# VectorE's side work of an iteration's second place behind the next iteration's q bias

## The chip, the cores and the metric

The kernel runs on one core of one Trainium2 chip. The metric is the device time of one execution in microseconds (us), lower is better. The time of the kernel before is 2167.18 us, the median of 3 runs (2166.52 to 2167.47). One more execution was taken by the hardware profiler; it took 2164.84 us, and its span, from the first to the last recorded instruction, is 2163.1 us.

## What is computed

One block of a network with adaptive layer norm: an attention-like layer and a mixture-of-experts layer, both with a residual, on 16 x 256 tokens of width 256, all in float32. What matters here, cut from the reference:

```python
h = _layernorm(x) * (1 + ca) + sa
q = (h @ q_w.T + q_b); k = (h @ k_w.T + k_b); v = (h @ v_w.T + v_b)   # 16 heads of 128
beta = softplus(h @ b_w.T + b_b)
qn, kn = _l2norm(q / scale), _l2norm(k / scale); gv = beta[..., None] * v
attn = einsum('bnhid,bnhjd->bnhij', qc, kc)                            # chunks of 64 tokens
out = einsum('bnhij,bnhjd->bnhid', attn * mask, gvc) * silu(h @ og_w.T)
x = x + ga * (out @ o_w.T + o_b)
h = _layernorm(x) * (1 + cb) + sb
scores = softmax(h @ gate_w.T); topk_w, topk_ids = lax.top_k(scores, 6)
x = x + gb * (sum over 16 experts of combine * swiglu(h) + shared swiglu(h))
```

## The kernel before

The tokens are cut into 32 tiles of 128, and 4 tiles make a supertile of 512. The 16 heads are cut into 4 groups of 4. The first phase, attention, is one loop over n = 0 to 127 (and two more turns to drain): iteration n treats one token tile t = n mod 4 of a supertile for one group of heads. The phase takes the first 1320 us or so. The second phase, experts, follows and is not touched.

Each engine has its own queue, in which the instructions stand in the order of the code, and semaphores join the queues. In iteration n TensorE does, in this order: the q projection of tile n (6 matmuls, 512 columns each), side work of the first place, the k projection, the output projection of the last supertile if t is 2, the scores of n-1 (`score(n - 1)`, into `s_ps`), the v projection, the attention product (`attend(n - 1)`, into `av_ps`), the transposes of q and k (`qt_ps`, `kt_ps`), side work of the second place, and, if t is 1, four gate projections (`project_gate`, 6 matmuls each). The q, k, v and gate products share two PSUM banks, `proj_ps0` and `proj_ps1`, in turn: `bank_free` makes each product wait until the one two before it has been read. So the v projection waits for the q bias, the second gate product waits for the v bias, and the third for ScalarE's silu of the first.

VectorE reads the products and adds the biases (`add_bias`, L1428: q, k, v), masks the scores (`mask`, L1434), makes the low part of the gated output (`lo_part`, L1457), the guarded sums of squares (`sum_squares`, L1441), and applies the gate (`apply_gate`, L1449). ScalarE squares q and k (L1117), copies the transposed q and k (L1108, L1110), makes the high part (`hi_part`, L1125, after L1449), and the silu of the gate products (L1131). GpSimd takes the inverse square root (L608) and scales q (L611) and v (L620).

Side work is what the main loop does not need at once: the layer norms of later supertiles, the preparation of later weights, and the routing for the experts. `plan()` puts it by a table of numbers into `side[n, 0]` and `side[n, 1]`, the first and the second place of iteration n, and each engine does its share of a task where its queue comes to that place. For VectorE the kinds with work of its own are, of the second places:

- `prep` and `tile` (a transposed piece of weights, 512 or 256 columns): TensorE transposes it into a PSUM bank, ScalarE copies the high part into `stage` (L1071), VectorE subtracts for the low part (L1335), waits for its own result and frees the bank, and SyncE stores the stage to memory (L398). There are two stage buffers, and the high part of a piece waits until the store of the piece two before it has landed.
- `stats`: `bn_stats` x4 (L1210), `bn_aggr` x4 (L1214), and an addition of eps (L1218), each waiting for the one before. GpSimd takes the inverse root (L592), and `norm` (L1227), in the first place of the next iteration, needs it.
- `x1` (L1284), the residual; `zturn` (L1250, L1256), the start of the softplus; `one` (L1261).

In the rows a tensor is named without its number: `q_sb`, `k_sb`, `v_sb` are the results of the biases, `scores<-s_ps` is the mask, and `proj_ps<-h_t,w_gate` a gate product.

Of the kernel before, what the change touches and what calls it, by code (L numbers as in the profile page):

```python
# [18 lines left out]
TS = ST // P  # L19
# [23 lines left out]
N = NI * TS  # L43
# [3 lines left out]
def after(eng, sem, count):  # L47
    if count > 0:
        eng.wait_ge(sem, count)


def f32(ap):
    return ap.bitcast(FP32)
# [81 lines left out]
def build(nc, x, q_w, q_b, k_w, k_b, v_w, v_b, b_w, b_b, og_w, o_w, o_b, gate_w, w13, w2, sw13, sw2, c, wmod, out):  # L135
    ctx = ExitStack()
    with ctx:
# [139 lines left out]
        side, late = plan()  # L277
# [921 lines left out]
        def _(dve):  # L1199
# [155 lines left out]
            n = KC * B  # L1355
# [14 lines left out]
            def boot_part(kind, h):  # L1370
                j = 2 * kind + h
                to = w_qkv[:, 0, kind, h] if kind < 3 else (w_gate if kind == G else w_out)[:, h]
                dve.wait_ge(boot_hi, j + 1)
                dve.tensor_tensor(to[:, 1, :], boot_ps[j][:, :], f32(to[:, 0, :]), ALU.subtract).then_inc(boot_lo, 1)
# [21 lines left out]
            def late_modulation():  # L1396
                dve.wait_ge(mod_turned, 2)
                dve.tensor_copy(mod[:, 4:12, :], s_ps[:, 2 * P:4 * P].rearrange("p (r d b) -> p r d b", r=8, d=2)[:, :, 0, :])\
                   .then_inc(gained, 1)
                dve.wait_ge(made, 3)  # L1400
                dve.wait_ge(gained, 3)
                gain = mod[:, CB * KC:(CB + 1) * KC, :]
                dve.tensor_scalar(gain, gain, 1.0, None, ALU.add).then_inc(gained, 1)
                steps = 4
                for w in (GA, GB):
                    m, s = mod[:, w * KC:(w + 1) * KC, :], sign[:, :, :]
                    dve.wait_ge(gained, steps)
                    dve.tensor_scalar(s, m, 0.0, 2.0, ALU.is_ge, ALU.mult).then_inc(gained, 1)
                    dve.wait_ge(gained, steps + 1)
                    dve.scalar_tensor_tensor(out=m, in0=m, scalar=-1.0, in1=m, op0=ALU.mult, op1=ALU.max).then_inc(gained, 1)  # L1410
                    dve.wait_ge(gained, steps + 2)
                    dve.tensor_scalar(m, m, 0.25, None, ALU.max).then_inc(gained, 1)
                    dve.wait_ge(gained, steps + 3)
                    dve.scalar_tensor_tensor(out=m, in0=s, scalar=-1.0, in1=m, op0=ALU.add, op1=ALU.mult).then_inc(gained, 1)
                    steps += 4
                dve.wait_ge(gained, steps)
                for h in range(KC):
                    dve.tensor_scalar(ga_ob[:, h, :], mod[:, GA * KC + h, :], o_b_sb[:, h:h + 1], None, ALU.mult)\
                       .then_inc(gained, 1)

            def add_bias(n, what):
                i, t = divmod(n, TS)
                if what == Q and n % 8 == 0:
                    dve.wait_ge(bias_loaded[(n // 8) % 2], 48 * (n // 16 + 1))
                dve.wait_ge(projected[what], n + 1)
                after(dve, (q_turned, k_turned, attended)[what], n - 1)
                at = (t + what) % 2
                dve.tensor_tensor(raw[what][t % 2][:, :], proj_ps[at][:, :], bias[:, (i // 2) % 2, what, :], ALU.add)\  # L1428
                   .then_inc(biased[what], 1)

            def mask(n):
                dve.wait_ge(scored, n)
                after(dve, attended, n - 1)
                dve.tensor_tensor(heads(scores[:, :]), heads(s_ps[:, :]),  # L1434
                                  causal[:, :].unsqueeze(1).broadcast_to([P, HG, P]), ALU.mult).then_inc(masked, 1)

            def sum_squares(n):
                dve.wait_ge(q_squared, n + 1)
                dve.wait_ge(k_squared, n + 1)
                after(dve, inverted, n - 1)  # L1440
                dve.tensor_scalar(guarded[n % 2][:, :], sumsq[n % 2][:, :], NORM_EPS2, None, ALU.max).then_inc(guard_done, 1)  # L1441

            def apply_gate(n):
                i, t = divmod(n - 1, TS)
                dve.wait_ge(attended, n)
                dve.wait_ge(gate_ready, HG * (i + 1))
                after(dve, gated_hi_done, n - 2)
                after(dve, gated_lo_done, n - 2)
                dve.tensor_tensor(gated[t % 2][:, :, :], heads(av_ps[:, :]), gate[:, :, t * P:(t + 1) * P], ALU.mult)\  # L1449
                   .then_inc(gated_done, 1)  # L1450

            def lo_part(n):
                i, t = divmod(n - 1, TS)
                at = slice(t * P, (t + 1) * P)
                dve.wait_ge(gated_hi_done, n)
                after(dve, out_projected, 2 * i)
                dve.tensor_tensor(gated_lo[:, :, at], gated[t % 2][:, :, :], f32(gated_hi[:, :, at]), ALU.subtract)\  # L1457
                   .then_inc(gated_lo_done, 1)

            def add_out(i, h):  # L1460
                g, a = group(i), i % 2
                dve.wait_ge(out_projected, 2 * i + h + 1)
                sums = acc[:, h, a * ST:(a + 1) * ST]
                if g == 0:
                    after(dve, delta_done, supertile(i) - 1)
                    dve.tensor_copy(sums, out_ps[:, :]).then_inc(added, 1)
                else:
                    dve.wait_ge(added, 2 * (i - 2) + h + 1)
                    dve.tensor_tensor(sums, out_ps[:, :], sums, ALU.add).then_inc(added, 1)
# [11 lines left out]
            def weigh(u):  # L1481
                w, a = divmod(u, 2)
                q, m = divmod(w, NM)
                dve.wait_ge(silu_done, u + 1)
                if m < ME:
                    if m == 0 and a == 0:
                        dve.wait_ge(comb_loaded[q % 2], 32 * (q // 2 + 1))
                    dve.tensor_tensor(silu_g[a][:, :], silu_g[a][:, :], combine[q % 2][:, a, :], ALU.mult)\
                       .then_inc(weighted, 1)

            def multiply(u):
                w, a = divmod(u, 2)
                q, m = divmod(w, NM)
                if m < ME:
                    dve.wait_ge(weighted, 2 * (q * ME + m) + a + 1)
                dve.wait_ge(u_done, u + 1)
                after(dve, hid_hi_done, u - 1)
                after(dve, hid_lo_done, u - 1)
                dve.tensor_tensor(hid[a], up_bank(u)[:, :], silu_g[a][:, :], ALU.mult).then_inc(hid_done, 1)  # L1499

            def lo_hidden(u):
                a = u % 2
                dve.wait_ge(hid_hi_done, u + 1)
                after(dve, downed, u - 1)
                dve.tensor_tensor(hid_lo[a], hid[a], f32(hid_hi[a]), ALU.subtract).then_inc(hid_lo_done, 1)

            for n in range(N + 2):
                i, t = divmod(n, TS)
                if n < N:
                    add_bias(n, Q)  # L1510
                    add_bias(n, K)
                if t == 2 and i:
                    add_out(i - 1, 0)
                if n == N + 1:
                    lo_hidden(0)
                if n >= 2:
                    mask(n - 1)
                if t != 2 and n >= 3:
                    lo_part(n - 2)
                if n >= N:  # L1520
                    weigh(n - N)
                if n < N:
                    for task in side[n, 0]:
                        do(task)
                    add_bias(n, V)
                    sum_squares(n)
                if t == 2 and i:
                    add_out(i - 1, 1)
                if n >= 2:
                    apply_gate(n - 1)  # L1530
                if n >= N:
                    multiply(n - N)
                if t == 1 and n >= 2:
                    lo_part(n - 1)
                if n == 1:
                    for h in range(KC):
                        boot_part(O, h)
                    late_modulation()
                if n < N:
                    for task in side[n, 1]:  # L1540
                        do(task)
                if n == 0:
                    for h in range(KC):
                        boot_part(G, h)
# [42 lines left out]
```

## Time and profile before

| | |
|---|---|
| median of 3 runs | 2167.18 us |
| profiled execution | 2164.84 us, span 2163.1 us |
| TensorE matmul busy | 2135.4 us, 99% of the span |
| TensorE weight load busy | 1752.6 us, 81% |
| VectorE busy | 1154.5 us, 53% |
| ScalarE busy | 1031.5 us, 48% |
| GpSimd busy | 522.2 us, 24% |
| granted TensorE clock | 1.0 of full speed (2.4 GHz) |

Busy time is what the instructions of an engine cover; matmuls are pipelined and overlap, so a busy TensorE may still have small holes in its rhythm. A time row reads: start, duration, engine, line, operation, what it writes and reads, count, and in brackets the idle time before it and what ended that. Where instructions follow each other without a wait, the next one starts before the recorded end of the one before (by some 0.08 us on VectorE), so the distance of two starts is what one really takes.

### The profile page before, as it was taken

The page shows a single profiled execution, that of the slowest core. Times are in us where ns is not written, and L with a number is a line of the kernel's source. Part 1 is how long each engine was busy: PE and PEld are TensorE (multiplying, and loading weights), DVE is VectorE, ACT ScalarE, POOL GpSimd, SP SyncE. Part 2 cuts the span into 40 slices and gives each one's busy share as a digit, 9 for nine tenths or more (in the row PEclk, how much of TensorE's full clock was granted, in tenths as well). Part 3 has the DMA queues.
Part 4 walks back from the last instruction along what each step waited for, and adds up shares of the span by engine and source line. Part 5 has one row for each costly group of instructions (what it writes and reads, how often), then busy time and mean ns, then how long its engine had stood idle before and what let it go on. Part 6 is the DMA issues. An engine that isn't in the chain of part 4 may idle for free.

```text
span 2163.1 us, 36173 instructions
## 1 busy us (share of the span) xinstructions
PE 2135.4 (99%) x12463; PEld 1752.6 (81%) x12463; DVE 1154.5 (53%) x2174; ACT 1031.5 (48%) x3300; POOL 522.2 (24%) x540
## 2 busy tenths in 40 slices
PE   8999999999999999999999999999999999999999
PEld 6778888888888887878888888888888888888887
DVE  6555654555555555555554445555555455545554
ACT  6655664665665665565565453333332333333232
POOL 2433443443443343343343441000000000000000
PEclk9999999999999999999999999999999999999999
DMA  8574443254355354354233221342334234323221
GB/s 264 185 239 133 146 138 123 81 162 139 93 145 159 84 154 136 95 147 142 106 143 113 70 107 49 129 170 98 127 125 149 88 121 156 103 97 113 96 94 63
DMA packets 191892, 274.79 MB, mean 127 GB/s; under 512 B 99184, under 2 KB 132960, under 8 KB 191712
## 3 DMA queue, kind: packets, MB, share of 16 engines
q1 hardware_dynamic: 191712, 272.49, 39.6%
q8 instruction: 101, 1.65, 0.3%
q14 instruction: 79, 0.65, 0.1%
HBM read 214.79 MB, written 57.67 MB: 126 GB/s over the span
## 4 chain that ended last, share of the span: by engine, by line
PE 92%; DVE 3%; ACT 2%; issue 2%; DMA 1%; DVEq 0%; POOL 0%; SPq 0%; ACTq 0%; POOLq 0%
PE proj_ps L651 49%; PE out_ps L651 14%; PE av_ps L877 5%; PE s_ps L866 4%; PE s_ps L924 3%; PE av_ps L924 3%; PE qt_ps L924 3%; PE kt_ps L924 3%; PE qt_ps L847 2%; PE kt_ps L852 2%; DMA head_scr<-stage 1%; PE misc_ps L670 1%; PE out_ps L721 0%; ACT squares L1117 0%; PE misc_ps L679 0%
## 5 line engine op out<-in xcount | busy, mean ns | idle before, releaser
L651 PE MATMUL proj_ps<-w_qkv,h_t 128*128 128x512 f32 x2304 | 618.0, 406 | 10.3 <-DVE q_sb L1428 2.1
L651 PEld LDWEIGHTS proj_ps<-w_qkv,h_t 128*128 128x128 f32 x2304 | 407.9, 188 | 103.3 <-issue 20.2
L651 PE MATMUL proj_ps<-h_t,w_qkv 128*128 128x512 f32 x1800 | 444.2, 391 | 0.3 <-issue 0.2
L651 PEld LDWEIGHTS proj_ps<-h_t,w_qkv 128*128 128x128 f32 x1800 | 335.6, 188 | 70.2 <-issue 1.3
L608 POOL TENSOR_TENSOR inv_norm<-guarded,minus_half 128x8 f32<-128x8 f32 x128 | 209.4, 1636 | 741.9 <-DVE guarded L1441 741.9
L1108 ACT ACTIVATE q_t<-qt_ps 128x512 f32<-128x512 f32 x128 | 76.3, 596 | 303.9 <-PE qt_ps L847 303.4
L651 PE MATMUL proj_ps<-h_t,w_gate 128*128 128x512 f32 x768 | 190.2, 398 | 2.6 <-ACT gate L1131 1.3
L1428 DVE TENSOR_TENSOR v_sb<-proj_ps,bias 128x512 f32<-128x512 f32 x128 | 88.5, 691 | 190.0 <-PE av_ps L877 183.4
L1117 ACT ACTIVATE squares<-q_sb 128x128 f32<-128x128 f32 x512 | 151.4, 297 | 56.9 <-DVE q_sb L1428 52.4
L1428 DVE TENSOR_TENSOR q_sb<-proj_ps,bias 128x512 f32<-128x512 f32 x128 | 88.4, 690 | 165.5 <-PE proj_ps L651 160.7
L651 PEld LDWEIGHTS proj_ps<-h_t,w_gate 128*128 128x128 f32 x768 | 139.8, 188 | 40.2 <-ACT gate L1131 10.7
L1117 ACT ACTIVATE squares<-k_sb 128x128 f32<-128x128 f32 x512 | 151.1, 297 | 19.8 <-DVE k_sb L1428 18.2
L651 PE MATMUL out_ps<-gated_hi,w_out 128*128 128x512 f32 x512 | 158.0, 390 | 0.1
L651 PE MATMUL out_ps<-h_t,w_qkv 128*128 128x512 f32 x594 | 150.9, 389 | 0.0
L1428 DVE TENSOR_TENSOR k_sb<-proj_ps,bias 128x512 f32<-128x512 f32 x128 | 88.4, 690 | 116.1 <-PE proj_ps L651 115.7
L877 PEld LDWEIGHTS av_ps<-scores,v_sb 128*128 128x128 f32 x1024 | 133.9, 191 | 10.7
L1151 ACT ACTIVATE w_gate<-v_sb 128x512 fp32r<-128x512 f32 x100 | 63.2, 632 | 161.8 <-DVE v_sb L1499 161.8
L1151 ACT ACTIVATE w_gate<-squares 128x512 fp32r<-128x512 f32 x100 | 63.2, 632 | 158.8 <-DVE squares L1499 154.6
L620 POOL TENSOR_TENSOR v_sb<-v_sb,v_scale 128x512 f32<-128x512 f32 x128 | 135.6, 1059 | 10.0
L611 POOL TENSOR_TENSOR q_sb<-q_sb,inv_norm 128x512 f32<-128x512 f32 x128 | 135.2, 1056 | 10.0
L877 PE MATMUL av_ps<-scores,v_sb 128*128 128x128 f32 x1024 | 134.7, 274 | 0.0
L651 PEld LDWEIGHTS out_ps<-h_t,w_qkv 128*128 128x128 f32 x594 | 111.5, 188 | 23.5
(216 smaller groups left out, 3174.5 us busy)
## 6 DMA issues: line engine op xcount, KB each, us to landing
w_qkv<-tile_scr SPq DMA_DIRECT2D x100, 768.0 KB, 4.3
w_qkv<-head_scr SPq DMA_DIRECT2D x45, 1024.0 KB, 11.0
head_scr<-stage SPq DMA_DIRECT2D x30, 512.0 KB, 3.8
w_gate<-head_scr SPq DMA_DIRECT2D x15, 1024.0 KB, 4.9
w_out<-head_scr SPq DMA_DIRECT2D x15, 1024.0 KB, 4.9
tile_scr<-stage SPq DMA_DIRECT2D x25, 512.0 KB, 3.1
x_in<-_attn_hidden_states_dram SPq DMA_DIRECT2D x16, 512.0 KB, 6.7
h_scr<-stage SPq DMA_DIRECT2D x16, 512.0 KB, 3.3
```

The lines of the kernel that those rows point to most:

```text
L608: pool.tensor_tensor(inv_norm[b][:, :], guarded[b][:, :], minus_half[:, :], ALU.pow).then_inc(inverted, 1)
L611: pool.tensor_tensor(q, q, inv_norm[b][:, 0:HG].unsqueeze(2).broadcast_to([P, HG, P]), ALU.mult)\
L620: pool.tensor_tensor(v, v, v_scale[b][:, :].unsqueeze(2).broadcast_to([P, HG, P]), ALU.mult)\
L651: mm = pe.matmul(out, w, y, start=(j == 0 and m == 0), stop=(3 * j + m == n - 1))
L847: mm = pe.transpose(qt_ps[:, h * P:(h + 1) * P], raw[Q][b][:, h * P:(h + 1) * P], ident)
L866: mm = pe.matmul(s_ps[c * CH:(c + 1) * CH, at], k_t[:, at], q_t[:, at], start=True, stop=True)
L877: mm = pe.matmul(av_ps[:, at], raw[V][(n - 1) % 2][:, at], scores[:, at], start=True, stop=True)
L924: mm = pe.matmul(y_ps[a][h][:, :], tiles_w[:, w % 4, r, at], y, start=(m == 0 and j == 0), stop=(m == NM - 1 and j == 2))
L1108: act.activation(q_t[:, :], qt_ps[:, :], ACT.Copy).then_inc(qt_copied, 1)
L1117: m = act.activation(squares[:, what, at], raw[what][n % 2][:, at], ACT.Square, accum_out=sumsq[n % 2][:, what * HG + h:what * HG + h + 1])
L1151: act.activation(hid_hi[u % 2], hid[u % 2], ACT.Copy).then_inc(hid_hi_done, 1)
L1428: dve.tensor_tensor(raw[what][t % 2][:, :], proj_ps[at][:, :], bias[:, (i // 2) % 2, what, :], ALU.add)\
```

## The change

VectorE's share of the second place of iteration n moves from the end of iteration n to the next iteration, between its q bias and its k bias, for all n from 2 to 126 but those with n mod 4 = 1. Nothing is added or taken away, and no other engine's order changes.

```diff
+            behind_q = lambda n: 2 <= n < N - 1 and n % TS != 1
             for n in range(N + 2):
                 i, t = divmod(n, TS)
                 if n < N:
                     add_bias(n, Q)
+                    if behind_q(n - 1):
+                        for task in side[n - 1, 1]:
+                            do(task)
                     add_bias(n, K)
...
-                if n < N:
+                if n < N and not behind_q(n):
                     for task in side[n, 1]:
                         do(task)
```

With the table as it is, 33 of the moved places hold work for VectorE: 10 a `prep` alone and one a `prep` with `one`, 3 a `tile`, 7 a `zturn`, 6 an `x1`, and 6 the `stats` of a routing norm, 5 of these with a `tile` behind it. The `stats` are those of n = 32, 40, 64, 72, 96 and 104, so their new place lies in iterations 33, 41, 65, 73, 97 and 105, which have t = 1 and so the gate products.

VectorE's queue from the end of iteration 40 into iteration 41, before:

```order
430 L1449 TENSOR_TENSOR gated<-av_ps,gate 128x512
431 L1210 BN_STATS stats<-x_in 128x6 x4
432 L1214 BN_AGGR mean_var<-stats 128x2 x4
433 L1218 TENSOR_SCALAR var_eps<-mean_var 128x4
434 L1335 TENSOR_TENSOR stage<-misc_ps,stage 128x256
435 L1428 TENSOR_TENSOR q_sb<-proj_ps,bias 128x512
436 L1428 TENSOR_TENSOR k_sb<-proj_ps,bias 128x512
437 L1434 TENSOR_TENSOR scores<-s_ps,causal 128x512
438 L1457 TENSOR_TENSOR gated_lo<-gated,gated_hi 128x4x128
439 L1227 TENSOR_SCALAR xn<-x_in,mean_var,rstd 128x256 x4
440 L1335 TENSOR_TENSOR stage<-out_ps,stage 128x512
441 L1428 TENSOR_TENSOR v_sb<-proj_ps,bias 128x512
```

The same place in the changed kernel:

```order
430 L1449 TENSOR_TENSOR gated<-av_ps,gate 128x512
431 L1428 TENSOR_TENSOR q_sb<-proj_ps,bias 128x512
432 L1210 BN_STATS stats<-x_in 128x6 x4
433 L1214 BN_AGGR mean_var<-stats 128x2 x4
434 L1218 TENSOR_SCALAR var_eps<-mean_var 128x4
435 L1335 TENSOR_TENSOR stage<-misc_ps,stage 128x256
436 L1428 TENSOR_TENSOR k_sb<-proj_ps,bias 128x512
437 L1434 TENSOR_TENSOR scores<-s_ps,causal 128x512
438 L1457 TENSOR_TENSOR gated_lo<-gated,gated_hi 128x4x128
439 L1227 TENSOR_SCALAR xn<-x_in,mean_var,rstd 128x256 x4
440 L1335 TENSOR_TENSOR stage<-out_ps,stage 128x512
441 L1428 TENSOR_TENSOR v_sb<-proj_ps,bias 128x512
```

The q bias moved ahead of the three steps of the statistics and the tile's low part, which now stand between it and the k bias.

The end of iteration 23 and the start of 24, where only a `prep` moves, before:

```order
268 L1449 TENSOR_TENSOR gated<-av_ps,gate 128x512
269 L1335 TENSOR_TENSOR stage<-misc_ps,stage 128x512
270 L1428 TENSOR_TENSOR q_sb<-proj_ps,bias 128x512
271 L1428 TENSOR_TENSOR k_sb<-proj_ps,bias 128x512
272 L1434 TENSOR_TENSOR scores<-s_ps,causal 128x512
```

And in the changed kernel:

```order
268 L1449 TENSOR_TENSOR gated<-av_ps,gate 128x512
269 L1428 TENSOR_TENSOR q_sb<-proj_ps,bias 128x512
270 L1335 TENSOR_TENSOR stage<-misc_ps,stage 128x512
271 L1428 TENSOR_TENSOR k_sb<-proj_ps,bias 128x512
272 L1434 TENSOR_TENSOR scores<-s_ps,causal 128x512
```

The q bias and the low part of the stage have changed places, and the rest stands as it was.

## Rows read from the trace of the kernel before

**Rows 1.** The page: busy time, share and count of each engine.
```profile
PE 2135.4 (99%) x12463; PEld 1752.6 (81%) x12463; DVE 1154.5 (53%) x2174; ACT 1031.5 (48%) x3300; POOL 522.2 (24%) x540
```
**Rows 2.** Waits of TensorE: who waited, for whom, us in total, times, longest.
```profile
PE proj_ps L651 <- DVE q_sb L1428: 2.1, 3, 1.1
```
**Rows 3.** Timeline of VectorE and TensorE around the start of iteration 24.
```profile
269.79 0.69 DVE L1335 TENSOR_TENSOR stage<-misc_ps,stage 128x512 fp32r<-128x512 f32 x1 [1.18 <-ACT stage L1071]
270.72 0.69 DVE L1428 TENSOR_TENSOR q_sb<-proj_ps,bias 128x512 f32<-128x512 f32 x1 [0.24 <-DVE stage L1335]
...
271.56 1.63 PE L651 MATMUL proj_ps<-w_qkv,h_t 128*128 128x512 f32 x6 [0.58 <-DVE q_sb L1428]
```
**Rows 4.** Timeline of VectorE, end of iteration 40 and iteration 41.
```profile
435.32 1.40 DVE L1210 BATCH_NORM_STATS2 stats<-x_in 128x6 f32<-128x256 f32 x4
...
437.16 0.51 DVE L1218 TENSOR_SCALAR var_eps<-mean_var 128x4 f32<-128x4 f32 x1
...
438.21 0.69 DVE L1428 TENSOR_TENSOR q_sb<-proj_ps,bias 128x512 f32<-128x512 f32 x1 [0.21 <-DVE stage L1335]
438.82 0.68 DVE L1428 TENSOR_TENSOR k_sb<-proj_ps,bias 128x512 f32<-128x512 f32 x1
...
442.80 0.69 DVE L1428 TENSOR_TENSOR v_sb<-proj_ps,bias 128x512 f32<-128x512 f32 x1 [0.21 <-DVE stage L1335]
```
**Rows 5.** Timeline of TensorE, iteration 41 and the start of 42.
```profile
436.64 0.60 PE L721 MATMUL out_ps<-ident,nat 128*128 128x128 f32 x4
...
438.57 0.69 PE L866 MATMUL s_ps<-q_t,k_t 128*64 128x64 f32 x16
...
440.68 1.05 PE L877 MATMUL av_ps<-scores,v_sb 128*128 128x128 f32 x8
...
442.36 1.17 PE L651 MATMUL proj_ps<-h_t,w_gate 128*128 128x512 f32 x4
...
448.26 1.07 PE L651 MATMUL proj_ps<-w_qkv,h_t 128*128 128x512 f32 x4
```
**Rows 6.** Timeline of ScalarE, iteration 41.
```profile
444.73 1.27 ACT L1131 ACTIVATE gate<-proj_ps 128x512 f32<-128x512 f32 x2
```
**Rows 7.** Timeline of GpSimd, iteration 41; lines L1218, L1256: ns min/median/max.
```profile
436.61 1.04 POOL L611 TENSOR_TENSOR q_sb<-q_sb,inv_norm 128x512 f32<-128x512 f32 x1
...
437.88 1.04 POOL L620 TENSOR_TENSOR v_sb<-v_sb,v_scale 128x512 f32<-128x512 f32 x1
...
L1218 DVE TENSOR_SCALAR var_eps<-mean_var x16: 169/170/506, 6.9 to 1482.9; 128x4 f32<-128x4 f32 x16
...
L1256 DVE SCALAR_TENSOR_TENSOR soft<-z x8: 225/226/1095, 20.6 to 954.5; 128x64 f32<-128x64 f32 x8
```
**Rows 8.** Timeline, statistics and side transposes of iterations 65 and 33.
```profile
680.61 1.40 DVE L1210 BATCH_NORM_STATS2 stats<-x_in 128x6 f32<-128x256 f32 x4
...
681.76 0.38 PE L721 MATMUL out_ps<-ident,nat 128*128 128x128 f32 x2
...
354.04 1.40 DVE L1210 BATCH_NORM_STATS2 stats<-x_in 128x6 f32<-128x256 f32 x4
...
354.75 0.60 PE L721 MATMUL out_ps<-ident,nat 128*128 128x128 f32 x4
```
**Rows 9.** Timeline of VectorE, TensorE, SyncE and ScalarE, iterations 7 to 9.
```profile
97.25 0.69 DVE L1335 TENSOR_TENSOR stage<-misc_ps,stage 128x512 fp32r<-128x512 f32 x1 [1.18 <-ACT stage L1071]
98.19 0.69 DVE L1428 TENSOR_TENSOR q_sb<-proj_ps,bias 128x512 f32<-128x512 f32 x1 [0.24 <-PE proj_ps L651]
...
97.89 0.60 PE L709 MATMUL out_ps<-ident,nat 128*128 128x128 f32 x4
...
98.02 0.33 SPq L398 DMA_DIRECT2D head_scr<-stage  x1
...
103.31 0.37 SPq L381 DMA_DIRECT2D w_gate<-head_scr  x1
...
110.16 0.60 ACT L1071 ACTIVATE stage<-out_ps 128x512 fp32r<-128x512 f32 x1 [3.03 <-DMA head_scr<-stage]
```

## The prediction

> **What bounds the kernel now.** I read the page first. TensorE's matmuls cover 99% of the span, VectorE's work 53% [rows 1]. So VectorE's order matters only where TensorE waits for it. The second view is TensorE's waits. Of the q bias, which the change lets go earlier, it has three waits, 2.1 us in all, the longest 1.1 [rows 2]. That is all that an earlier q bias can give back: 0.1% of the time. The third view is the timeline around the moved places, since what is late there after the change is no wait yet.
>
> **Where the q bias is late now.** At the start of iteration 24 the low part of a stage waits 1.18 us for ScalarE, runs from 269.79, and the q bias follows only at 270.72. The v projection, which needs its bank, starts at 271.56 after 0.58 us of idle time [rows 3]. This pair gives two prices. A low part holds the queue for 0.93 us up to the next bias (its length and the wait for its own end before it frees the bank). And TensorE starts 0.84 us after the start of the VectorE instruction that releases it.
>
> **The prep and tile places (14), x1 (6), zturn (7).** A q bias that finds VectorE free starts about 0.3 us after its projection ends: the side transposes behind the projection of iteration 8 start at 97.89, the bias at 98.19 [rows 9]; I take 0.25. In iteration 41 the q projection ends at 436.64 and the k projection at 438.57 [rows 5], 1.93 us apart with side transposes between. In this gap fit the q bias (0.61, the distance of two biases, 438.21 to 438.82, [rows 4]) and a low part of 0.93. The k bias is then on time, or, where no transposes stand in the gap or the high part is late, up to 0.3 late. It may be 0.56 late at no cost: on time, at 438.57 + 0.11, its mask would start at 439.28, and the attention product at 440.68 [rows 5] needs it only by 440.68 - 0.84 = 439.84. So in the low-part places nothing is lost on TensorE by the k bias. Iteration 24 gains the 0.58, iteration 16, by the same pattern, I take as 0.2. Sum -0.8, bounds 0 and -2.1. x1 is an instruction of a low part's shape, and zturn is shorter; both cost nothing, as they fit in the gap.
>
> For zturn a row speaks against that. Its second step (L1256) took 0.23 in the median, but once 1.09 us [rows 7]. After the move it stands where GpSimd scales q, and if it waits each time for that (1.04 us, [rows 7]) the k bias is up to 0.1 later than the slack allows: 7 times 0.1, 0.7 us, the upper bound. I take 0. The Trainium skill ("SBUF — State Buffer", "Who interferes with whom") says that a VectorE instruction with two inputs in SBUF waits out a GpSimd instruction that reads SBUF and started first. By that rule, the wait would come in all seven; the 1.09 agrees with it.
>
> **The six statistics places.** Here lies the cost. At the end of iteration 40 VectorE is free at 435.32 and uses the time in which TensorE still does the q projection: the statistics start at 435.32, and statistics and low part are done when the q bias starts at 438.21, 2.89 us later [rows 4]. The q bias is already 1.3 late, but it costs TensorE nothing: the v projection runs on time. After the change VectorE has nothing to do from 435.32 until the q projection's end plus 0.25, 436.89: it idles 1.57 us, and then has the same work to do before the v bias. From 435.32 to the v bias at 442.80 its queue is full but for two waits of 0.21 for its own results [rows 4]. So the v bias comes 1.57 us later, less what the work itself gets shorter.
>
> It does get shorter by one item. The addition of eps took 0.51 us at 437.16, against a median of 0.17 [rows 7]; it ended at 437.67, when GpSimd's scaling of q, started at 436.61, ended (437.65). In its new place it starts at 436.89 + 0.61 + 1.84 = 439.34 (1.84 from 435.32 to 437.16), and GpSimd's next long one has ended at 438.92 [rows 7]. That saves 0.34.
>
> What hangs on it on TensorE: first the attention product. New mask: 436.89 + 0.61 + (2.89 - 0.34) + 0.60 = 440.65, so the product starts at 441.49 instead of 440.68, 0.8 late. Then the gate products. They start at 442.36 and the next iteration at 448.26 [rows 5]: 5.90 for four, 1.47 each if none waits, and the third would start at 445.30. But the third needs the bank that ScalarE's silu of the first reads, and that hangs on a chain: v bias 442.80, sums of squares, gate, ScalarE's high part, silu at 444.73 for 0.64 [rows 6], which is 445.37. So the end of iteration 41 hangs on the v bias with no slack, and moves by its whole 1.57 - 0.34 = 1.23 us. The 0.8 of the attention product is inside that and not added.
>
> The other five by the same count. Idle time added, from the start of the statistics to the start of the side transposes plus 0.25 [rows 8]: iteration 65 has 1.40, 33 has 0.96; 73 is like 65, and 97 and 105 like 41. Sum 3 x 1.57 + 2 x 1.40 + 0.96 = 8.5. Less 5 x 0.34; in 33 the eps meets GpSimd's scaling of v again and I count 0.2: 1.9. Net +6.6. Bounds: 8.5 if nothing is saved; 4.6 if only the attention product waits (3 x 0.8, 2 x 0.87, 0.46).
>
> **The stores behind the moved low parts.** SyncE's queue is in order. The low part of iteration 7's prep starts at 97.25 now, and behind the q bias it starts at 98.19 + 0.61 = 98.80, 1.55 later. Its store (98.02) goes with it, so does the w_gate load at 103.31, which waits for the store to land, and the store behind that load; ScalarE in iteration 9 waited 3.03 us, until 110.16, for a stage buffer [rows 9]. It would wait until 111.7, and with it v bias and gate products of iteration 9: +1.5. The other preps move by 0 to 0.5, since their low parts wait for the high part anyway, as in [rows 3]; one more chain of this kind, in iteration 13, I take as +0.5. Sum +2.0, bounds 0 (a store lands faster when fewer transfers are beside it) and +4. No other engine's order changes; the phase of the experts, 840 us, is as before.
>
> **Sum.** -0.8 + 6.6 + 2.0 = +7.8 us. Against its own time, 2164.84 for the profiled execution, that is 2172.6. That execution is 2.3 below the median of the runs; on the median of 2167.18 the forecast is 2175.0 us, 0.36% slower. What a measurement of this kernel can tell from no change is about 0.2%, 4.3 us: slower means above 2171.5, faster below 2162.8.
>
> **Rivals.**
> - *The freed q bias is all that counts (not slower).* If the gate products do not hang on the v bias, and the attention product has more slack than I read, the statistics cost nothing and the waits of [rows 2] go: -1.2 with the stores at 0, 2166.0; at most -2.1, 2165.1. For it: a q bias 1.3 late costs nothing now, so a late k bias may also. Against: the k bias would be 436.89 + 0.61 + 2.55 = 440.05, 1.37 late against a slack of 0.56, and the mask stands directly behind it. It decides from side work of under 1.8 us in the gap; the statistics with a tile have 2.55. 0.15, of which 0.03 is faster.
> - *Only the attention product waits.* The third gate product has slack that the merged rows hide: 4.6 instead of 6.6, stores and gains as before or less, +4 to +6; 2172 on the median. For it: that the third product waits for the silu is worked out, not read. 0.17.
> - *The stage stores pile up.* In the first 280 us the two stage buffers are turned twice an iteration, and TensorE also waits for weights there. If each of the 11 moved preps hands on a delay, +4 more than forecast, and eps saves nothing, +1.9: +14, 2181. Against: only one low part moves by more than 0.5. 0.10.
> - The forecast, +6 to +10: 0.58.
>
> Faster 0.03, within 0.2% 0.20 (the rest of the first, and 0.08 of the second and of the forecast's lower edge), slower 0.77. Range 2169.0 to 2179.0: below it lie the first rival, above it the worst of the third.
>
> **What the new profile would show.** Right: in iteration 41 and its five like, TensorE's attention product waits 0.5 to 0.9 us for the mask, a wait that the list of waits does not have now, and the gate products wait for ScalarE's silu; VectorE idles about 1.5 us before the q bias there; the eps addition is 0.17 in five of six; the 0.58 of iteration 24 is gone; in iteration 9 ScalarE waits some 4.5 us for its stage. Wrong: the v bias of iteration 41 not later than its q projection by 1.2 more than now; or the gate products not moved by it; or a second phase that changes by more than 0.5 us.

## The result, and the profile after

The changed kernel takes 2172.59 us (median of 8 runs, 2172.11 to 2173.72), the kernel before 2166.20 us in the same runs (median of 8, 2164.82 to 2167.47). The ratio is 1.0031, with a 95% interval of 1.0020 to 1.0041: 6.4 us slower (+4.3 to +8.9 by the interval), which the scatter of the runs does not explain. The forecast was +7.8 us and 2175.0 us; on this median of the kernel before it would be 2174.0. The profiled execution of the changed kernel took 2172.43 us (span 2170.7).

The page after, the same line as [rows 1]; nothing in it says why the kernel is slower:

```profile
PE 2136.8 (98%) x12463; PEld 1751.3 (81%) x12463; DVE 1154.1 (53%) x2174; ACT 1031.1 (48%) x3300; POOL 522.5 (24%) x540
```

The waits of TensorE say more (the changed kernel; who waited, for whom, us in total, times, longest):

```profile
PE proj_ps L651 <- ACT gate L1131: 3.3, 11, 1.2
PE av_ps L877 <- DVE scores L1434: 2.8, 5, 0.6
PE proj_ps L651 <- DMA w_qkv<-head_scr: 1.6, 1, 1.6
...
PE proj_ps L651 <- DVE q_sb L1428: 1.1, 1, 1.1
```

Of the 2.1 us of waits for the q bias in [rows 2], 1.1 are left, the one of the start-up. In their place stand five waits of the attention product for the mask, which were not in the list before, and 3.3 us for the silu of the gate products. Before, that line was:

```profile
PE proj_ps L651 <- ACT gate L1131: 1.3, 6, 0.4
```

Most of the growth on that line lies elsewhere: 1.8 of the 3.3 us are two waits in iterations 9 and 13, and four of the six statistics iterations (33, 41, 73, 97) have one of 0.16 to 0.18 us each. The list shows only a wait of over 0.15 us, and from the recorded end of the matmuls before, so what the silu costs has to be read from distances of starts, below.

The timeline of VectorE in iteration 41, the answer to [rows 4] (start, duration):

```profile
438.66 0.69 DVE L1428 TENSOR_TENSOR q_sb<-proj_ps,bias 128x512 f32<-128x512 f32 x1 [1.43 <-PE proj_ps L651]
439.27 1.40 DVE L1210 BATCH_NORM_STATS2 stats<-x_in 128x6 f32<-128x256 f32 x4
440.70 0.38 DVE L1214 BATCH_NORM_AGGREGATE mean_var<-stats 128x2 f32<-128x6 f32 x4
441.12 0.17 DVE L1218 TENSOR_SCALAR var_eps<-mean_var 128x4 f32<-128x4 f32 x1
441.19 0.42 DVE L1335 TENSOR_TENSOR stage<-misc_ps,stage 128x256 fp32r<-128x256 f32 x1
441.82 0.69 DVE L1428 TENSOR_TENSOR k_sb<-proj_ps,bias 128x512 f32<-128x512 f32 x1 [0.21 <-DVE stage L1335]
442.43 0.68 DVE L1434 TENSOR_TENSOR scores<-s_ps,causal 128x512 f32<-128x512 f32 x1
...
445.82 0.69 DVE L1428 TENSOR_TENSOR v_sb<-proj_ps,bias 128x512 f32<-128x512 f32 x1 [0.21 <-DVE stage L1335]
```

VectorE idles 1.43 us before the q bias (1.5 by the distance of starts), in the time in which it did the statistics before. The eps addition takes 0.17 us now, not 0.51, since no GpSimd instruction lies over it. And from the start of the statistics to the v bias the queue is full again.

TensorE in the same iteration, the answer to [rows 5]:

```profile
438.46 0.60 PE L721 MATMUL out_ps<-ident,nat 128*128 128x128 f32 x4
...
440.39 0.69 PE L866 MATMUL s_ps<-q_t,k_t 128*64 128x64 f32 x16
...
443.17 1.16 PE L877 MATMUL av_ps<-scores,v_sb 128*128 128x128 f32 x8 [0.50 <-DVE scores L1434]
...
444.96 3.27 PE L651 MATMUL proj_ps<-h_t,w_gate 128*128 128x512 f32 x12
448.39 3.02 PE L651 MATMUL proj_ps<-h_t,w_gate 128*128 128x512 f32 x12 [0.16 <-ACT gate L1131]
451.24 1.07 PE L651 MATMUL proj_ps<-w_qkv,h_t 128*128 128x512 f32 x4
```

From the side transposes behind the q projection to the first product of the next iteration it was 448.26 - 436.64 = 11.62 us, and it is 451.24 - 438.46 = 12.78: 1.16 us more in this one iteration. Of these, the attention product has 0.67 before its start (443.17 - 440.39 = 2.78, against 440.68 - 438.57 = 2.11) and 0.11 from there to the first gate product (1.79 against 1.68), and the four gate products have 0.38 (451.24 - 444.96 = 6.28, against 448.26 - 442.36 = 5.90). Note that the bracket of the attention product says 0.50 and not 0.67: an idle time is counted from the recorded end of the matmuls before, which overlap.

What held the gate products can be read from single matmuls. The second product of the changed kernel, and the third product of the kernel before (each from a window that opens inside it; the count is that of the window), are:

```profile
446.57 1.66 PE L651 MATMUL proj_ps<-h_t,w_gate 128*128 128x512 f32 x6
```

```profile
445.37 1.45 PE L651 MATMUL proj_ps<-h_t,w_gate 128*128 128x512 f32 x5
```

The second product starts 446.57 - 445.82 = 0.75 us after the start of the v bias, and 0.38 us after the matmul before it, where two matmuls of one product are 0.23 apart. The third starts 448.39 - 447.75 = 0.64 us after the start of the silu:

```profile
447.75 1.11 ACT L1131 ACTIVATE gate<-proj_ps 128x512 f32<-128x512 f32 x2
```

In the kernel before it was 445.37 - 444.73 = 0.64 too, and 0.39 after the matmul before it. In all six statistics iterations of both kernels the silu starts 1.93 us after the v bias, and the third product 0.63 to 0.64 after the silu. So the third product hung on the v bias with no slack before the change and does so after it.

The same difference can be taken for every iteration: how much later the scores of the iteration after it start than before. The steps over 0.08 us are these (us, positive is later), each profile against that of the kernel before:

| step behind iteration | changed kernel | only statistics (e2) | without statistics (e1) |
|---|---|---|---|
| 1 (start-up, no place moved) | -0.90 | -0.13 | 0 |
| 7 to 9 | +1.41 | +0.46 | +1.28 |
| 12 and 13 | +1.25 | +1.02 | -0.48 |
| 15, 16 | -0.06 | 0 | -0.13 |
| 24 | -0.61 | 0 | -0.61 |
| 33 | +0.67 | +0.68 | 0 |
| 41 | +1.17 | +1.16 | 0 |
| 65 | +1.00 | +1.01 | 0 |
| 73 | +1.06 | +1.06 | 0 |
| 97 | +1.29 | +1.24 | 0 |
| 105 | +1.19 | +1.20 | 0 |

The six statistics places have 6.4 us, and behind iteration 105 the distance stays as it is to the end of the phase. The profiled executions as a whole are 7.6 us apart. The other 1.2 us come before iteration 25: +1.8 up to iteration 13, where e2, still equal to the kernel before, has +1.4, and -0.6 in iteration 24.

### The profile page after: what moved, and what is told of

It is laid out like the page before. It is cut to its first block, busy times and chain, and to the rows that moved or that the text cites. A ratio compares the mean times of both kernels' runs of the same rounds, so it can differ in the third digit from the quotient of the medians.

```text
span 2170.7 us, 36173 instructions
## 1 busy us (share of the span) xinstructions
PE 2136.8 (98%) x12463; PEld 1751.3 (81%) x12463; DVE 1154.1 (53%) x2174; ACT 1031.1 (48%) x3300; POOL 522.5 (24%) x540
## 4 chain that ended last, share of the span: by engine, by line
PE 89%; DVE 4%; ACT 2%; issue 2%; DMA 1%; SPq 0%; DVEq 0%; ACTq 0%
PE proj_ps L651 48%; PE out_ps L651 14%; PE av_ps L877 5%; PE s_ps L866 3%; PE s_ps L924 3%; PE av_ps L924 3%; PE qt_ps L924 3%; PE kt_ps L924 3%; PE qt_ps L847 2%; PE kt_ps L852 2%; DMA head_scr<-stage 1%; PE misc_ps L670 1%; ACT gate L1131 1%; DVE stage L1335 0%; DVE xn L1227 0%
```

## The experiments

The theory to test: the loss lies in the six statistics places alone. VectorE idles there before the q bias and does the work after it, in front of the k bias, the mask and the v bias, and the gate products hang on the v bias over a chain. Rivals: any side work between q and k bias costs something; the loss is in the stores of the first 280 us; only the mask is waited for.

**e1, without the statistics places.**

```diff
-            behind_q = lambda n: 2 <= n < N - 1 and n % TS != 1
+            behind_q = lambda n: 2 <= n < N - 1 and n % TS != 1 and not any(task[0] == "stats" for task in side[n, 1])
```

> The changed kernel with the six places that hold the statistics left where they were before; the other 27 moved. My theory: all but about 1.4 us of the loss (the stores behind the moved low parts, less the freed q bias) goes, and the attention products of iterations 33, 41, 65, 73, 97, 105 wait for no mask: 0 to +2.5 us against before. A rival, that any side work between the q bias and the k bias costs something, says at least +4.

Measured: 2165.30 us against 2165.74 of the kernel before, ratio 0.9996 (0.9988 to 1.0005). The loss is gone with the six places; the other 27 moved places together cost nothing that can be measured, in the median 0.4 us less than before (-2.6 to +1.1), a little below the 0 to +2.5 that I expected. The rival's +4 lies outside the interval, and no wait of the attention product for the mask is in the list.

**e2, the statistics places alone.**

```diff
+            behind_q = lambda n: 2 <= n < N - 1 and any(task[0] == "stats" for task in side[n, 1])
```

> Only the six statistics places are moved (n = 32, 40, 64, 72, 96, 104), everything else as before. My theory: +6.4 us against before, of which iteration 33 has 0.7 and the others 1.0 to 1.3 each, and nothing before 350 us. The rival that the loss is in the stores of the first 280 us says under +3.

Measured: 2171.90 us against 2165.74, ratio 1.0028 (1.0017 to 1.0039), +6.2 us. The table above shows the same six steps as in the changed kernel, each within 0.05 us. One part of the expectation missed: the profile has steps of +1.5 us behind iterations 7 to 13 too, where this kernel is word for word the kernel before. More on this under e5.

**e6, only the tile behind the q bias.** In five of the places the statistics stay, and the tile's low part moves:

```diff
+            behind_q = lambda n, task: 2 <= n < N - 1 and task[0] == "tile" and side[n, 1][0][0] == "stats"
...
+                    for task in side.get((n - 1, 1), ()):
+                        if behind_q(n - 1, task):
+                            do(task)
                     add_bias(n, K)
...
                     for task in side[n, 1]:
-                        do(task)
+                        if not behind_q(n, task):
+                            do(task)
```

> In five of the six places the statistics stay at the end of the iteration and only the tile's low part goes behind the q bias; everything else as before. My theory (VectorE loses time only where it idles before the q bias, and the k bias may be 0.56 us late): VectorE idles nowhere, the queue up to the v bias is as full as before, 0 us, within 0.5 of before. The rival that a late k bias costs by itself says +0.5 us per place, +2.5.

Measured: 2165.45 us against 2165.74, ratio 1.0000 (0.9991 to 1.0008). Its VectorE timeline in iteration 41:

```profile
435.69 1.39 DVE L1210 BATCH_NORM_STATS2 stats<-x_in 128x6 f32<-128x256 f32 x4
...
437.95 0.68 DVE L1428 TENSOR_TENSOR q_sb<-proj_ps,bias 128x512 f32<-128x512 f32 x1
438.55 0.41 DVE L1335 TENSOR_TENSOR stage<-misc_ps,stage 128x256 fp32r<-128x256 f32 x1
439.17 0.69 DVE L1428 TENSOR_TENSOR k_sb<-proj_ps,bias 128x512 f32<-128x512 f32 x1 [0.21 <-PE proj_ps L651]
...
443.17 0.69 DVE L1428 TENSOR_TENSOR v_sb<-proj_ps,bias 128x512 f32<-128x512 f32 x1 [0.21 <-DVE stage L1335]
```

From the statistics to the v bias it is 443.17 - 435.69 = 7.48 us, as before (442.80 - 435.32 = 7.48, [rows 4]). So a low part behind the q bias costs nothing as long as the queue stays full ahead of it. The run says nothing of a late k bias: against the end of the q projection the k bias starts here at 439.17 - 437.01 = 2.16 us, and in the kernel before at 438.82 - 436.64 = 2.18, so it did not get later, and the rival of the expectation was not put to the test.

**e3, the chain behind the v bias, taken by itself.** The kernel before, with the silu of the first gate product ahead of the high part on ScalarE:

```diff
+                first = 1 if t == 1 and 2 <= n < N else 0
+                if first:
+                    silu_gate(i, 0)
                 if n >= 2:
                     hi_part(n - 1)
...
-                    for h in range(HG):
+                    for h in range(first, HG):
                         silu_gate(i, h)
```

> The kernel before, with one other change: in the iterations with gate products (t = 1, n of 5 and more) ScalarE does the silu of the first gate product ahead of the high part, not behind it. My theory says that the third gate product waits on the chain v bias, gate, high part, silu, not only in the six places but by about 0.3 us in most of these iterations (5.82 us for four products in the middle, 5.53 at best). Then this takes 0.54 us out of the chain, and the kernel gets faster by 31 x 0.3 = 9 us at most, 5 to 9 us. If the gate products are not bound by that chain, nothing changes (within 1 us).

Measured: 2160.10 us against 2165.74, ratio 0.9974 (0.9964 to 0.9985): 5.6 us faster. The chain from the v bias over gate, high part and silu is real, and held TensorE in the kernel before as well. It held it in fewer iterations than the 31 I had multiplied: the profile has steps of -0.2 to -0.4 us behind 33, 37, 41, 45, 65, 69, 73, 77, 97, 101, 105 and 109, where VectorE has side work ahead of the v bias, and next to none in the others. These are 4.3 us, which is what the two profiled executions differ by; the rest of the 5.6 is not seen in the one profile. That the total fell into the range of 5 to 9 us is in part luck, since 31 iterations were counted on and 12 gained.

**e4, the changed kernel with e3's edit.**

> The changed kernel together with the silu of the first gate product ahead of the high part. If the gate products hang on v bias, gate, high part and silu in the statistics iterations, the freed 0.54 us is partly usable there too: each is then bound by the attention product (+0.8) and by the second gate product's wait for the v bias (+0.3), so +1.1 each against the kernel with the silu first alone, 6 us in all, 2166 us; a wait of the gate products for the v bias appears in their place. If they hung on the attention product alone, the loss would be 4.6.

Measured: 2165.19 us against 2165.33, ratio 0.9999 (0.9990 to 1.0008). e3 ran in another session; each against its own kernel before, this one is 5.5 us above e3. Step by step against e3's profile: 0.51, 1.08, 0.85, 0.90, 1.15 and 1.07 in the six iterations, 5.6 in sum, against 6.4 without the edit. So part of the loss hung on the silu, as the theory says, and the larger part comes by the attention product. The wait for the v bias that I expected in its place is not in the list of waits, but it shows in the starts. TensorE in iteration 41, and below it the second product by itself:

```profile
440.98 1.16 PE L877 MATMUL av_ps<-scores,v_sb 128*128 128x128 f32 x8 [0.51 <-DVE scores L1437]
...
442.76 6.00 PE L651 MATMUL proj_ps<-h_t,w_gate 128*128 128x512 f32 x24
448.61 1.52 PE L651 MATMUL proj_ps<-w_qkv,h_t 128*128 128x512 f32 x6
```

```profile
444.37 1.43 PE L651 MATMUL proj_ps<-h_t,w_gate 128*128 128x512 f32 x5
```

The row of 24 gate matmuls covers 6.00 us here and 5.70 in the iterations of this kernel that have no side work. The v bias started at 443.62, and the second product starts 0.75 us later, at 444.37, as in the changed kernel. It starts 0.37 us after the matmul before it, where e3 has 0.23 at the same place. Iterations 65 and 73 have no such wait (0.88 us after the v bias, 0.23 to 0.24 apart), and of the five with a tile they are the two with the smaller steps, 0.85 and 0.90.

**e5, the stores alone.**

```diff
+            behind_q = lambda n: n in (6, 7, 10, 11)
```

> Only the places of n = 6, 7, 10 and 11 are moved, four prep places whose q bias costs TensorE nothing now, so nothing can be gained: this measures the cost of later stores alone. The term of the prediction says +2.0 us. The other theory, after the kernel without the statistics places came out 0.4 us below before and a kernel with none of these places moved showed its iteration 14 later by 1.4 us all the same, is that later stores are within what the landing times of one execution vary by: under +1 in the median, though the w_qkv load of iteration 8 then waits about 1 us longer in the profile.

Measured: 2165.93 us against 2165.33, ratio 1.0003 (0.9994 to 1.0012). The 0.6 us can't be told from nothing, and it is under my term of +2.0 us; but the interval, -1.3 to +2.6 us, holds the +2.0 too, so this run alone does not refute it. In the waits of TensorE the w_qkv load shows, 0.25 us before:

```profile
PE proj_ps L651 <- DMA w_qkv<-head_scr: 1.2, 1, 1.2
```

But this wait also moves by itself. In the changed kernel it is 1.6 us, in e1 1.4, in e4 1.0; where these four preps are not moved, it is 1.2 in e7, 0.7 in e2, 0.3 in e6, and in e3 and e8 not in the list. One profile can't weigh such a term. The ten profiles together say a little: the v projection of iteration 8, which needs the load, starts between 101.02 and 101.72 in the four kernels with these preps moved, and between 100.05 and 100.94 in the six without. The stage of iteration 9 comes free at 110.9 in the mean of the four and at 110.4 in that of the six, and the scores of iteration 15 start 0.3 to 0.5 us later (0.3 without e8, which also has another order on VectorE; single kernels scatter by over 2 us). So the later stores do seem to delay the load, and the cost that they leave is of the size of e5's 0.6 us.

**e7 and e8, versions meant to beat both.** e7 has e3's edit and moves only the places whose q bias was late:

```diff
+            behind_q = lambda n: n in (12, 15, 23)
```

> A version meant to beat both: the kernel before with the silu of the first gate product first, and of the moved places only n = 12, 15 and 23, where the q bias is late now. My theory: the silu's 5.6 us and 0.6 + 0.2 + 0.5 us from the three places: 2159.0 us, 1 us under the silu alone, hardly outside its noise. In the profile the waits of TensorE for the q bias in iterations 13 and 24 are gone.

Measured: 2159.63 us against 2165.33, ratio 0.9971 (0.9960 to 0.9981). The step of iteration 24 against e3 is -0.62 us and the waits for the q bias go from 2.2 to 1.1 us; in time it is 5.7 us under its kernel before, where e3, from another session, was 5.6 under its own, so the forecast 1 us under e3 is not seen. e8 has on top of it the gate ahead of the sums of squares in the iterations with gate products:

```diff
                     add_bias(n, V)
-                    sum_squares(n)
+                    if t != 1:
+                        sum_squares(n)
...
                     apply_gate(n - 1)
+                if n < N and t == 1:
+                    sum_squares(n)
```

> The same, and in the iterations with gate products VectorE applies the gate ahead of the guarded sums of squares. The sums of squares wait for ScalarE's squares in iterations 9 and 13 (0.8 us each), and take 0.07 elsewhere. Theory: 1 to 2 us below the same kernel without it if the chain from gate to silu still binds there, else the same.

Measured: 2158.72 us against 2165.33, ratio 0.9968 (0.9956 to 0.9981), 0.9 us under e7 in the median. Its step behind iteration 9 is -0.67 us against e7, where the expectation had 0.8; iteration 13 shows -0.20, and with the landing times as they vary neither is shown by one profile, nor does the time tell e8 from e7, so the expected 1 to 2 us are not shown. Both versions are faster than the kernel before, by 5.7 and 6.6 us, and nearly all of it is e3's edit.

## Why the prediction was right

- *What bounds the kernel.* Right: 1.0 us of q-bias waits went, and no more was to be had.
- *The low parts, x1 and zturn cost nothing by the k bias.* Right: e1. In iteration 24 the v projection now starts 0.61 us after the scores, without a wait (272.05 and 272.66), where [rows 3] has 0.58 of idle time:

```profile
272.05 0.69 PE L866 MATMUL s_ps<-q_t,k_t 128*64 128x64 f32 x16
272.66 1.66 PE L651 MATMUL proj_ps<-w_qkv,h_t 128*128 128x512 f32 x6
```

  The forecast gain of this place was 0.58; its step is -0.61. The k bias came late, at 272.45, and was absorbed.
- *zturn waits for GpSimd.* It does, and it costs nothing. The second step has a median of 0.41 us now, 0.23 before [rows 7]:

```profile
L1256 DVE SCALAR_TENSOR_TENSOR soft<-z x8: 227/410/415, 19.7 to 960.3; 128x64 f32<-128x64 f32 x8
```

  The rule of the Trainium skill that the prediction draws on ("SBUF — State Buffer", "Who interferes with whom") agrees with this row: all seven wait. The wait is about 0.2 us and not a whole scaling of 1.04, since in the changed kernel each starts some 0.7 us into the scaling of q (at 549.13 in iteration 51, the scaling at 548.42) and ends with it. No step shows in these seven iterations.
- *The statistics places.* Right in place, mechanism and size: forecast 0.76, 1.23, 1.06, 1.06, 1.23, 1.23 (6.6 in all), seen 0.67, 1.17, 1.00, 1.06, 1.29, 1.19 (6.4), and +6.2 in e2's runs. From the q projection's end to the v bias, iteration 41 has 445.82 - 438.46 = 7.36 us, against 442.80 - 436.64 = 6.16: 1.20 later, where 1.23 was forecast. The attention product was 0.67 late and not 0.8: the distance of 0.84 us from a bias to the product that it releases was read at iteration 24, and from the mask to the attention product it is 443.17 - 442.43 = 0.74. The saving at the eps addition came in all six (0.25 us in iteration 33, 0.33 in the others). The line in the changed kernel has 259 ns at most, where [rows 7] has 506:

```profile
L1218 DVE TENSOR_SCALAR var_eps<-mean_var x16: 169/170/259, 6.8 to 1490.5; 128x4 f32<-128x4 f32 x16
```

- *The stores.* Probably too high. The term was +2.0 us, and e5 has +0.6 (-1.3 to +2.6 by its interval); e1 has -0.4 (-2.6 to +1.1) with the gains of some 0.8 in it, which leaves 0.4 for the stores. So e5 does not exclude +2.0, and e1, by its upper end, puts the stores at +1.9 at most. The reason given for the lower bound, that a store lands faster when fewer transfers are beside it, is shown by no run. The count "ScalarE's wait goes from 3.0 to 4.5 us in iteration 9" failed in the changed kernel's profile too: the stage came free at 110.70, not 111.7, after 3.27 us. (That execution was 1.1 us ahead at the q bias of iteration 8, at 97.11 against 98.19; from there to the free stage it took 13.6 us against 12.0, as much more as I had counted, but e7, where this prep is not moved, took 13.5.)

```profile
110.70 0.60 ACT L1071 ACTIVATE stage<-out_ps 128x512 fp32r<-128x512 f32 x1 [3.27 <-DMA head_scr<-stage]
```

  I had shifted one landing by the delay of its store and left the rest of the transfer times as they were in one execution. The 1.6 us that TensorE waited for the w_qkv load in iteration 8 there were not in the count either. With this term at 0.6 the sum is 6.4, the measured median. That it fits to the tenth is luck, since the interval of the result spans 4.6 us, and holds +7.8 as well.
- *The rivals.* "Only the attention product waits" fell, since the iterations lost 1.0 to 1.3 and not 0.8, and since e4 lost less than the changed kernel. It was nearer than I gave it, though: 0.67 of the 1.16 in iteration 41 comes by the mask. In full, with the 0.11 up to the first gate product, it is 0.78. "Not slower" fell by e2, and "the stores pile up", which needs +6 from them, by e5 and e1.

That the gate products wait for the silu is shown by e3 in time, and that the silu hangs on the v bias by the equal distances (1.93 and 0.64 us) in the six iterations before and after. How the loss divides between mask and v bias is read from the profiles and, in part, from e4; no run moves one of them alone.

## What to carry to other kernels

An instruction moved behind one that waits does not only go later: the engine also stands idle in front of that wait, and if its queue is full from there to the next thing that another engine needs, the whole idle time comes out at the end, less what the moved work itself gets shorter. So for each moved piece compare its length with the time until the wait ends at its old place, and with the slack at its new place: 0.9 us behind the q bias fitted and was free, 2.6 us did not and cost 1.0 to 1.3 (0.7 in iteration 33, where no tile stands behind the statistics and the idle time was 0.8). Look for the slack on all chains that start there (here mask to attention product, and v bias, gate, silu to the third gate product); the one found this way was worth 5.6 us when shortened by itself.

## What the runs showed of the hardware

- An eps addition of 4 columns took 0.51 us beside a scaling on GpSimd and 0.17 without one. In its new place it took 0.17 in five of the six iterations and 0.26 in the sixth. So work that meets a GpSimd instruction can get shorter by being later.
- TensorE's progress through the first 170 us differs by up to 1.5 us between executions of kernels that are equal there (the wait for w_qkv in iteration 8 is 1.2 us in e7 and too short for the list in e3, and the start-up step runs from -0.90 to 0), while the steps of the six statistics iterations repeat within 0.05 us, and from the last scores to the end all ten profiles take 840.6 to 840.7 us. In these profiles the scatter of the time is in the start, not in the middle.
- TensorE started a product 0.73 to 0.75 us after the start of the 128x512 VectorE instruction that it waited for (mask to attention product, v bias to second gate product), and 0.84 in the q bias of iteration 24; after ScalarE's silu, 0.63 to 0.64.
